# Decays ahead of the weight's late splits in the first state-space sequence, and attention's out projection as three fp32r parts

## The reference, cut to what matters

```python
# layer 1: state space, D_INNER = 1024, 16 heads of 64, state 64
zxbcdt = X @ W_in.T                          # z, x, B, C, dt
dt  = softplus(dt + dt_bias)
xBC = silu(causal_conv4(xBC) + conv_b)       # x, B and C, 1152 channels
h_t = h_{t-1} * exp(dt * A) + dt * B x ;  y_t = h_t C + D x
out1 = rmsnorm(y * silu(z)) @ W_out.T + X    # then a layer norm

# layer 2: attention, 16 heads of 32, context of 512 tokens
q, k, v = x @ Wq.T + bq, ctx @ Wk.T + bk, ctx @ Wv.T + bv
out2 = softmax(q k.T * scale) v @ Wo.T + bo  # then a residual and a layer norm
```

## Time and profile before

| | us |
|---|---|
| median of 3 runs | 2155.63 (2154.73 to 2157.56) |
| the profiled execution's own time | 2156.37 |
| its span, first to last instruction | 2154.6 |
| mean granted clock of PE | 0.967 of full speed |

### The profile page before, as it was taken

One profiled execution on the slowest core, in us unless ns is written; L12 is line 12 of the kernel. 1 busy time (PEld: TensorE's weight loads), 2 busy tenths in 40 slices (PEclk: granted clock), 3 DMA queues, 4 the chain that ended last, 5 costly groups with the idle time before them and its releaser, 6 DMA issues. The chain is left out here.

```text
span 2154.6 us, 39863 instructions
## 1 busy us (share of the span) xinstructions
PE 2001.9 (93%) x13356; PEld 1318.8 (61%) x13356; DVE 1414.4 (66%) x2811; ACT 1223.3 (57%) x3068; POOL 389.6 (18%) x595
## 2 busy tenths in 40 slices
PE   6999999999999999858999999999999999689988
PEld 4767676767676767434555555555655564378853
DVE  6978787878787868535556565656565656265438
ACT  4435353444444444217868787877777777246514
POOL 0111101111111110231212212122222222100006
PEclk8999999999999999888999999999999999889999
DMA  6122222222222222242333232334343322161157
GB/s 205 53 58 78 59 77 59 77 53 82 49 87 49 87 47 69 79 127 80 98 81 113 75 111 69 118 81 118 80 113 82 100 82 70 66 233 59 59 177 272
DMA packets 120289, 200.94 MB, mean 93 GB/s; under 512 B 22945, under 2 KB 44449, under 8 KB 120097
## 3 DMA queue, kind: packets, MB, share of 16 engines
q1 hardware_dynamic: 110880, 179.46, 27.4%
q0 software_dynamic: 9216, 18.89, 3.5%
HBM read 117.53 MB, written 29.88 MB: 68 GB/s over the span
## 5 line engine op out<-in xcount | busy, mean ns | idle before, releaser
L1579 ACT ACTIVATE a_shared<-a_shared,a_mx 128x512 f32<-128x512 f32 x512 | 340.8, 669 | 50.6 <-DVE a_mx L1627 50.5
L1572 ACT ACTIVATE a_probs<-a_scores 128x512 f32<-128x512 f32 x512 | 291.9, 603 | 109.6 <-PE a_scores L1730 107.3
L1627 DVE TENSOR_REDUCE a_mx<-a_shared 128x1 f32<-128x512 f32 x512 | 318.3, 681 | 30.2 <-PE a_shared L1714 29.8
L925 PE MATMUL m_proj<-m_xt_hi,link 128*128 128x512 f32 x576 | 245.2, 426 | 21.2 <-DVE m_xt_lo L649 10.5
L1730 PE MATMUL a_scores<-a_qs,a_ks 98*128 98x512 f32 x512 | 217.7, 434 | 21.5 <-ACT a_probs L1572 17.7
L1714 PE MATMUL a_shared<-a_ks,a_qs 96*128 96x512 f32 x512 | 220.2, 441 | 15.8 <-ACT a_shared L1579 11.6
L926 PE MATMUL m_proj<-m_xt_lo,link 128*128 128x512 f32 x576 | 233.2, 405 | 0.0
L927 PE MATMUL m_proj<-m_xt_hi,link 128*128 128x512 f32 x576 | 232.1, 403 | 0.0
L1067 PE MATMUL m_outp<-m_wout,m_g 128*128 128x512 f32 x512 | 226.0, 600 | 2.7 <-issue 2.7
L1688 PE MATMUL a_shared<-link 128*128 128x512 f32 x768 | 189.8, 400 | 18.5 <-POOL a_ks L1519 15.7
L460 ACT ACTIVATE m_acc<-m_proj,m_cb,m_cw 128x512 f32<-128x512 f32 x72 | 58.1, 818 | 254.4 <-PE m_proj L927 253.7
(11 more groups left out here) (243 smaller groups left out, 3327.2 us busy)
## 6 DMA issues: line engine op xcount, KB each, us to landing
m_dec<-step_decay SPq DMA_DIRECT2D x64, 256.0 KB, 4.0
a_qs<-link SPq DMA_DIRECT2D x256, 64.0 KB, 2.1
m_ce<-run_decay SPq DMA_DIRECT2D x128, 112.0 KB, 3.6
a_ks<-a_k_hi POOLq DMA_DIRECT2D x192, 64.0 KB, 2.4
e_x<-x SPq DMA_DIRECT2D x11, 1024.0 KB, 5.6
m_xt_in<-x_t_in SPq DMA_DIRECT2D x8, 1024.0 KB, 8.1
m_x_tok<-x_in SPq DMA_DIRECT2D x8, 1024.0 KB, 6.5
x<-m_x_tok SPq DMA_DIRECT2D x32, 256.0 KB, 2.2
```

The source lines that it names most:

```text
L925: pe.matmul(bank[:, :], wh, xt_hi[:, k, :], start=(k == 0), stop=False)
L1572: act.activation(probs[:, n % 2, h, :], scores[t.score_bank(n, h)][:, :], ACT.Exp, scale=-1.0).then_inc(exp_ready, 1)
L1579: act.activation(scored[:, :], scored[:, :], ACT.Exp, scale=-1.0, bias=mx[:, i % 2, j, h:h + 1], accum_out=den[:, i, j, h:h + 1]).then_inc ...
L1627: dve.tensor_reduce(mx[:, i % 2, j, h:h + 1], bank(what)[:, :], AX.X, ALU.min).then_inc(mx_ready, 1)
```

## The change

In the state-space stage, for the first sequence alone: SP stores the decays as soon as they are there, without waiting for all eight splits; each load of step decays waits until the chunk staged in its buffer is split (`DEC_CHUNK + gr + 1`). Chunk 7 is staged in chunk 2's place, and is loaded when three chunks are split. On DVE the convolution of x tile 1 comes before the running decays, splits 3 and 4 stay in the head, 5 comes behind the convolutions of group 1, 6 and 7 stand in group 1, and `local_decays` of groups 1, 2 and 3 stand in groups 0, 1 and 2. B and C use accumulator 1 in every sequence, and in the first one ACT does x tile 0's first tap before the silus of B and C.

In the attention stage: `o` and Wo are split into high and low fp32r parts, and an out tile is twelve fp32r matmuls. `norm` writes back into `inv_rows`, and a new DVE step `osplit` adds bv and makes the two parts of a group of `o`, behind unit 1 (last group of the sequence before), 6, 10 and 14. Wo is loaded into `x_tok` and split on DVE in units 2, 3, 6 and 7 of the first turn. bv is no longer added to v. The scratch for dynamic DMAs is set to 2048.

```diff
-                  *(dec_flat[:, n * narrow:(n + 1) * narrow] for n in range(4)), g_flat[:, 0:narrow]]
+                  *(dec_flat[:, n * narrow:(n + 1) * narrow] for n in range(4)),
+                  g_flat[:, wide + narrow:wide + 2 * narrow]]
...
+        DEC_CHUNK = 3
...
                 if gr >= 2:
                     sp.wait_ge(m_ready, at(b, NG, gr - 1))
+                if first:
+                    sp.wait_ge(w_used, DEC_CHUNK + gr + 1)
...
-                sp.wait_ge(w_used, 1)
+                sp.wait_ge(w_used, DEC_CHUNK)
                 load_columns(len(CHUNKS) - 1)
                 load_residual(b, True)
                 sp.wait_ge(w_in[0], 16)
                 sp.dma_start(wout[:, :, :], woutT.rearrange("(c p) n -> p c n", p=P)).then_inc(w_in[0], 16)
-
-                sp.wait_ge(w_used, len(CHUNKS))
                 store_decays(b)
                 load_decays(b, True)
...
-                conv_tap0(b, 8, 1, 0)
+                conv_tap0(b, 8, 1, 1)
...
+                if first:
+                    x_tap0(b, True, 0)
                 act.wait_ge(conv_read, at(b, 9, 1))
...
-                act.activation(bt[:, :], acc[0:NS, 0, :], ACT.Silu)
+                act.activation(bt[:, :], acc[0:NS, 1, :], ACT.Silu)
...
-                for n in range(2):
-                    x_tap0(b, first, n)
+                if not first:
+                    x_tap0(b, False, 0)
+                x_tap0(b, first, 1)
...
-                conv(b, 8, 1, 0, 1)
+                conv(b, 8, 1, 1, 1)
                 softplus(b)
                 step_sizes(b, True)
                 conv(b, 0, 2, 0, 2)
+                conv(b, 1, 3, 1, 3)
                 running_decays(b, True)
-                conv(b, 1, 3, 1, 3)
-                for c in range(3, len(CHUNKS)):
+                for c in (3, 4):
                     split_columns(c)
                 head_weights(b)
                 head_products(b)
                 scaled_x(b, True, 0)
                 local_decays(b, 0)
                 next_convs(b, 0)
-                local_decays(b, 1)
+                split_columns(5)
                 carried_factors(b, 0)
...
                     if gr:
                         next_convs(b, gr)
+                        if first and gr == 1:
+                            for c in (6, 7):
+                                split_columns(c)
...
-                    if first and gr < 2:
-                        local_decays(b, 2 + gr)
+                    if first and gr + 1 < NG:
+                        local_decays(b, 1 + gr)
...
+WO_UNITS = [2, 3, 6, 7]
...
+        if u == (2 if n >= TT else 1):
+            put("osplit", group, 0, 0, d)
...
-                sp.dma_start(w_o[:, :, :], woT.rearrange("(k p) n -> p k n", p=P)).then_inc(small_in, 16)
+                sp.dma_start(brow[:, :], b_row[1].partition_broadcast(P)).then_inc(small_in, 16)
+                sp.dma_start(bvcol[:, :], b_row[0]).then_inc(small_in, 16)
+                sp.dma_start(x_tok[:, :, :], woT.rearrange("(k p) n -> p k n", p=P)).then_inc(small_in, 16)
...
                 elif kind == "load":
+                    if t.first():
+                        sp.wait_ge(wo_s, 2 * KT)
...
-                    dve.tensor_tensor(v[:, i, :], bank(what)[:, :], brow[:, 0, :], ALU.add).then_inc(v_ready, 1)
+                    dve.tensor_copy(v[:, i, :], bank(what)[:, :]).then_inc(v_ready, 1)
...
+                    dve.tensor_tensor(inv_rows[:, :], o_bank[:, :], inv_rows[:, :], ALU.mult).then_inc(o_ready, 1)
+                elif kind == "osplit":
                     if i == 0 and not t.first():
                         dve.wait_ge(out_done, t.at(TT, 0))
-                    dve.tensor_tensor(o[:, i, :], o_bank[:, :], inv_rows[:, :], ALU.mult).then_inc(o_ready, 1)
+                    dve.wait_ge(o_ready, t.at(KT, i + 1))
+                    dve.tensor_scalar(o_hi[:, i, :], inv_rows[:, :], bvcol[:, i:i + 1], None, ALU.add
+                                      ).then_inc(o_split, 1)
+                    dve.wait_ge(o_split, t.at(2 * KT, 2 * i + 1))
+                    dve.scalar_tensor_tensor(out=o_lo[:, i, :], in0=inv_rows[:, :], scalar=bvcol[:, i:i + 1],
+                                             in1=o_hi[:, i, :].bitcast(F32), op0=ALU.add, op1=ALU.subtract
+                                             ).then_inc(o_split, 1)
+                elif kind == "wo":
+                    dve.wait_ge(small_in, N_SMALL)
+                    dve.tensor_copy(wo_hi[:, i, :], x_tok[:, i, :]).then_inc(wo_s, 1)
+                    dve.wait_ge(wo_s, 2 * i + 1)
+                    dve.tensor_tensor(wo_lo[:, i, :], x_tok[:, i, :], wo_hi[:, i, :].bitcast(F32), ALU.subtract
+                                      ).then_inc(wo_s, 1)
...
-                        pe.wait_ge(o_ready, t.at(KT, KT))
+                        pe.wait_ge(wo_s, 2 * KT)
+                        pe.wait_ge(o_split, t.at(2 * KT, 2 * KT))
                     take(part, what, t)
                     for k in range(KT):
-                        ins = pe.matmul(bank(what)[:, :], o[:, k, tile], w_o[:, k, :], start=(k == 0),
-                                        stop=(k == KT - 1))
+                        for n, (op, wp) in enumerate(((o_hi, wo_hi), (o_hi, wo_lo), (o_lo, wo_hi))):
+                            ins = pe.matmul(bank(what)[:, :], op[:, k, tile], wp[:, k, :], start=(k == n == 0),
+                                            stop=(k == KT - 1 and n == 2))
...
-    nc = bacc.Bacc("TRN2", target_bir_lowering=False, num_devices=1)
+    nc = bacc.Bacc("TRN2", target_bir_lowering=False, num_devices=1, dynamic_dma_scratch_size=2048)
```

More of the change, by code:

```diff
@@ L474, in x_tap0 @@
                 if n == 0:
-                    act.wait_ge(bc_ready, at(b, 1, 1))
-                elif n == 1:
                     if not first:
                         act.wait_ge(xc_ready, at(b, XT_TILES, 0))
+                elif n == 1:
+                    act.wait_ge(bc_ready, at(b, 1, 1))
                 else:
@@ L567, in head @@
                     act.wait_ge(ce_ready, at(b, NG, 0))
-                act.activation(bt[:, :], acc[0:NS, 0, :], ACT.Silu)
-                act.activation(ct[0:NS, :], acc[NS:P, 0, :], ACT.Silu)
-                act.activation(ct[NS:P, :], acc[NS:P, 0, :], ACT.Silu).then_inc(bc_ready, 1)
-                for n in range(2):
-                    x_tap0(b, first, n)
+                act.activation(bt[:, :], acc[0:NS, 1, :], ACT.Silu)
+                act.activation(ct[0:NS, :], acc[NS:P, 1, :], ACT.Silu)
+                act.activation(ct[NS:P, :], acc[NS:P, 1, :], ACT.Silu).then_inc(bc_ready, 1)
+                if not first:
+                    x_tap0(b, False, 0)
+                x_tap0(b, first, 1)
                 if not first:
@@ L852, in groups @@
                     if gr + 1 == NG and more:
-                        conv(b + 1, 8, 1, 0, 1)
+                        conv(b + 1, 8, 1, 1, 1)
                     skip_added(b, first, gr, 0)
@@ L1260, in parts_of @@
     first = [(name + (0, 0, 0))[:4] for name in first]
+    first_turn = []
+    for step, d in steps:
+        if d >= 0:
+            first_turn.append((step, d))
+        if d == 0 and step[0] == "st" and step[3] == AG - 1 and TT * step[1] + step[2] in WO_UNITS:
+            first_turn.append((("wo", WO_UNITS.index(TT * step[1] + step[2]), 0, 0), 0))
     return {"start": [(step, 0) for step in first + [step for step in start if step not in first]],
-            "first": [(step, d) for step, d in steps if d >= 0],
+            "first": first_turn,
             "steady": steps,
@@ L1334, in attention_stage @@
         w_lo = {n: kept[i][1] for i, n in enumerate(names)}
-        w_o = sb("wo", [P, KT, DM])
-        brow = sb("brow", [P, 2, DM])
+        wo_hi = sb("wo_hi", [P, KT, DM], F32R)
+        wo_lo = sb("wo_lo", [P, KT, DM], F32R)
+        brow = sb("brow", [P, DM])
+        bvcol = sb("bvcol", [P, KT])
         ident = sb("ident", [P, P])
@@ L1356, in attention_stage @@
         inv_rows = sb("inv_rows", [P, SEQ])
-        o = sb("o", [P, KT, SEQ])
+        o_hi = sb("o_hi", [P, KT, SEQ], F32R)
+        o_lo = sb("o_lo", [P, KT, SEQ], F32R)
         stats = sb("stats", [P, TT, 6])
@@ L1369, in attention_stage @@
         small_in = sem("small_in")
+        wo_s = sem("wo_s")
+        o_split = sem("o_split")
         const = sem("const")
@@ L1455, in load_rest @@
             def load_rest():
-                for i in range(2):
-                    sp.dma_start(brow[:, i, :], b_row[i].partition_broadcast(P)).then_inc(small_in, 16)
-                sp.dma_start(w_o[:, :, :], woT.rearrange("(k p) n -> p k n", p=P)).then_inc(small_in, 16)
+                sp.dma_start(brow[:, :], b_row[1].partition_broadcast(P)).then_inc(small_in, 16)
+                sp.dma_start(bvcol[:, :], b_row[0]).then_inc(small_in, 16)
+                sp.dma_start(x_tok[:, :, :], woT.rearrange("(k p) n -> p k n", p=P)).then_inc(small_in, 16)
             def load_x(t, n):
```

(8 more changed lines are left out.)

## The result

The changed kernel takes 2135.24 us (median of 4 runs, 2132.66 to 2138.33) against 2155.18 us for the kernel before beside it (median of 4, 2151.86 to 2157.56): ratio 0.9905, 95% interval 0.9884 to 0.9926. Measured once more, beside the last experiments, it was 2139.66 us against 2158.58, ratio 0.9917 (0.9903 to 0.9931). By medians and by ratios the gain is 18 to 20 us.

The account below looks back on a forecast made before the run. PE was taken as the bound in attention, with DVE and PE both close in the first state-space sequence from 68 us. 5.8 + 14 + 1.5 - 0.5 = 20.8 us off 2156.4 gave 2135.6, so 2135; range 2129 to 2142.

Parts of the forecast that it names:

- Earlier start, store, gap: First state-space sequence: earlier tap gains 1.9 us; decays stored at 29.3, scan at 36.9, DVE gap 1.1 of 4.99, gain 3.9.
- Step 3: SP's queue, first sequence: last weight columns, residual and W_out load later; costed at nothing, store 1 us later as a bound.
- step 2: Store of the running decays, first sequence: at 29.3 us, including 0.4 for the second convolution's tap; gain 3.9 us.
- POOL's product blocks split 5: First sequence: split 5 stands for POOL's W_out product as the scans did; no change, 2.7 us gained or lost as bounds.
- Group 3: First sequence: PE's wait for DVE before local outputs grows from 1.05 to some 4 us; they start some 6 us earlier.
- The rival that the 10.9 us stay: First sequence passes in full: DVE's other idle time takes the moved work; 2130 us, chance 0.12.
- Steady sequences, 2.0 us each: Attention: 2.7 us saved by out tiles less 0.7 for DVE's splits, 2.0 kept in each of seven sequences, 14 us.
- out projection in full: Rival, attention: ACT catches up and nothing of 2.7 us a sequence is lost, 5 us more; 2130 us, chance 0.18.
- ACT takes it back: Rival, attention: PE only waits longer for the exponentials, steady sequences keep nothing; 2149 us, chance 0.17.
- POOL's queue: Rival: smaller scratch makes each dynamic DMA wait for the one before, 28 us over eight sequences; 2163 us, chance 0.03.
- The tail, 1.5 us gained: Eighth out projection, where nothing hides: 1.3 us of splits added, 4 x 0.7 saved, 1.5 us gained.
- Clock, 1 us off: First sequence: a longer wait before the local outputs can halve PE's clock; 1 us taken off the gain.

Follow-up runs that it names:

- the repetition: The changed kernel measured once more, unaltered, beside the last experiments: 2139.66 us, ratio 0.9917 to the kernel before.
- run 8: Changed kernel with ACT's first tap of x tile 0 back behind the B and C silus: 2143.25 us, 0.9929 of the kernel before.
- run 10: Changed kernel with last o split in unit 0, PE's wait for o block by block, W_out's product in two halves: 2135.15 us, 0.9890 of before.
- run 5: Changed kernel with POOL's W_out product moved behind the last scaled x of the first sequence: 2144.61 us, 0.9940 of the kernel before.
- run 3: Changed kernel with the last group's split of o moved from unit 1 to unit 0: 2136.55 us, 0.9910 of the kernel before.
- Run 4: Changed kernel with PE's wait for o's parts taken block by block in the first out tile: 2138.08 us, 0.9910 of the kernel before.
- run 6: Changed kernel with both operations of each split of o done twice: 2173.76 us, 1.0076 of the kernel before.
- run 9: Changed kernel with last o split in unit 0 and PE's wait for o block by block: 2137.45 us, 0.9895 of the kernel before.

## Why the prediction was right, and where not

The total was forecast at 2135 us and came out at 2135.24. Step by step:

- **Earlier start, store, gap.** Right. Store 29.36 against 29.3; first scan 37.54 against 36.9; gap 1.49 against 1.1. That the store fits to 0.1 us is luck: in the eleven profiles with the tap early it stands at 28.4 to 29.9 us, 28.42 in the repetition. From the store's issue to the scan it took 8.2 us, not 7.6, and that lies between the store and the first load: 3.51 us (29.36 to 32.87) where it was 2.75. Step 3 (costed at nothing, 1 us as a bound) would have W_out's load as the cause, and this load did land at 30.0, behind the store's issue. But in run 8 it landed at 30.3, ahead of the store at 31.11, and store to load still took 3.6 us. So the cause stays open. Run 8 shows the tap to be on the path. One slip in the sum: step 2 charges 0.4 us to the second convolution, and 1.9 + 3.9 leaves it out; DVE's waits for the tap and for the loads shrank by 5.0 us (1.93 + 4.99 to 0.42 + 1.49).
- **POOL's product blocks split 5.** Right to 0.1 us: 2.69 us lost (3.38 for 0.69), and run 10, which takes it away, starts group 3 two microseconds earlier. It was a cost that the change could have shed; the prediction only moved it.
- **Group 3.** Wait "some 4 us", 3.99 to 4.00 in all twelve profiles that have the state-space part. Local outputs "some 6 us earlier": 6.7, 5.8 in the repetition. The mark came 6.3 and 5.2 us earlier, forecast 5.8. The clock fell as said, 3.32 us for 64 products. The rival that the 10.9 us stay is out. My reason for the wait was incomplete (run 5).
- **Out tiles.** 2.80 us against 2.82 forecast, from 3.49: 0.69 us saved a tile, 2.8 a sequence. With the one wait for DVE taken away run 3 keeps 2.4 of them (111.4 to 109.0). The Trainium skill (FP8 and Floating Point Precision, TensorE Precision Notes) has true FP32 as four passes through the array; three parts for four passes of equal length would be 0.87 us a tile, 3.5 a sequence, an estimate. The traces show the passes not to be of equal length (0.218 us for one of fp32, 0.233 for an fp32r matmul), and bear out the rows.
- **Steady sequences, 2.0 us each.** Right, a little high: 669.25 - 658.42 = 10.8 and 11.1 us over six, the seventh 2.2 and 1.75, so 13 where 14 was forecast. Unit 1 cost 0.36 against 0.5 (the wait, 0.53 for 0.17). Neither "out projection in full" nor "ACT takes it back" happened, though the wait in which the loss shows has ACT as its releaser.
- **W_o's splits, 0.5 lost.** Nothing: 146.59 against 146.63 us.
- **POOL's queue.** Out: 192 issues of `a_ks` at 0.50 us each, as in the earlier trace rows.
- **The tail, 1.5 us gained. This step failed.** It lost 0.33. The 1.3 us of splits were there (2.24 for 0.88), and the other three tiles saved 1.9 us of their 2.1. The sum left out that the longer wait halves PE's clock at the first tile, which begins 5.43 us ahead of the second, where 4.55 less 0.69 makes 3.9. I had costed that for group 3 and not here. Run 4 takes the wait away and gets 3.7 us.
- **Clock, 1 us off.** For group 3 right. Not foreseen is how much it moves elsewhere. Two sequences of the changed kernel's profile, the fourth and the fifth, are alike in every start up to here (PE behind group 3's local outputs, 108 us apart):

```profile
426.09 0.50 PE L933 MATMUL m_proj<-m_xt_hi,link 128*128 128x512 f32 x1 [0.20 <-DVE m_xt_lo L654]
426.43 0.40 PE L934 MATMUL m_proj<-m_xt_lo,link 128*128 128x512 f32 x1
...
533.92 0.80 PE L933 MATMUL m_proj<-m_xt_hi,link 128*128 128x512 f32 x1 [0.20 <-DVE m_xt_lo L654]
534.52 0.63 PE L934 MATMUL m_proj<-m_xt_lo,link 128*128 128x512 f32 x1
```

  The same pause of 1.05 us goes before both, ahead of group 3's local outputs at 423.68 and 531.51. In the second the next seven matmuls run at 1.2 GHz and the sequence is 1.45 us longer. Of fourteen profiles four (after, runs 3, 6 and 9) have sequences 2 to 4 without this drop, always those three together, and ten have it in all. That is 4.4 us, and the runs of one kernel lie 4 to 14 us apart. So the agreement to 0.2 us is luck: the profile's span shrank by 18.9 us where the terms sum to 20.8, and its execution was 2.2 us above the median. The terms, within 2 us each, are what was right.

## What to carry to other kernels

An engine that is busy two thirds of the time hides added work only place by place: 1.25 us ahead of six maxima cost 0.36 us of PE's time, in an idle stretch one unit earlier nothing, and doubled everywhere 34 us in all, of which the place ahead of the maxima was nearly half. Where a part of an operand is late, wait for it at its own matmul and not at the first; in the tail that was 3.7 us, since PE kept its clock too, though no total shows it. Before moving work into an idle stretch, look at what runs on the engine just ahead of the stretch, and who waits for that.

## What the runs showed that I had not expected

- A wait of 2.24 us in the tail and one of 1.85 us in run 6's first steady sequence both put PE at half clock, but the same wait of 1.84 us two sequences later did not (clock 1.00); waits of 1.05 and 1.33 us did so in some sequences and not, or much shorter, in others, of the same code. After the 1.33 us wait it lasted 2 us in one kernel and over 11 in another.
- DVE's operations on SBUF that meet POOL's product of 7.02 us are held until it ends, however much of it is left: the cast of split 5 ends at 49.05 with the product ending at 48.50 (3.38 us for 0.69), and run 5's first gate product at 103.81 with the product ending at 103.27 (7.07 for 0.68). POOL's sums of squares did the same to two subtractions in run 5 (1.75 us each for 0.68). DVE's convolutions, which read PSUM, stayed at 4.53 us for six beside the product; so two halves of 3.60 us beside convolutions held up nothing (run 10).
